# Cross-attention of a decoder layer: matmul operands padded with zeros to the full array

## Chip, cores and metric

One core of a Trainium2 chip runs the whole program. The metric is the device time in microseconds (us) of one execution; lower is better. The engines of the core run side by side and wait for each other through semaphores: TensorE (PE in the profile, its weight loads PEld), VectorE (DVE), ScalarE (ACT), GpSimd (POOL) and SyncE (SP), which issues the DMAs.

## The reference, cut to what matters

A decoder layer over 64 sequences of 128 rows and 128 features: causal self-attention, cross-attention over a context of 77 rows, and a mixture-of-experts FFN, each behind a layer norm and a residual. The change touches the cross-attention only (16 heads of 8 features):

```
Q, K, V = heads of query @ Wq.T + bq, context @ Wk.T + bk, context @ Wv.T + bv
qk      = Q @ K.T                                 # 128 x 77 per head
scores  = qk / sqrt(8)
feats   = mean(scores), mean of the row maxima, mean variance of softmax(scores)
t       = exp(clip(mlp(feats)))                   # one temperature per sequence and head
attn    = softmax(qk / (2 t))
out     = (attn @ V) @ Wo.T + bo
```

## The kernel before

The program has three stages one after the other, with a barrier between them: `self_attention`, `cross_attention` and `expert_ffn`. X, the activations of all sequences, stays on the chip. The cross stage runs a software pipeline that is unrolled: `for n in STEPS`, n from -3 to 77, the same loop on every engine, and each call in it is guarded by `real(b)`, that is 0 <= b < 64. In step n the early part works on sequence n (projections a step or two ahead), and the late part on sequence n - 11 (`LAG`), because a group of 8 sequences must pass the temperature MLP before its second softmax can start. The order on an engine is the order in which the code is written; semaphores alone tie the engines.

The parts of a step that the change touches, on TensorE:

- `scores_outer`, `scores_inner` (L1033): queries as weights, masked keys as moving data, in row groups of 32 (four heads of 8 features). They fill `SQ` with qk for the statistics.
- `subtract_max` (L1063): three more matmuls add minus the row maximum of each head onto `SQ`. Weights are `mT` (16 heads x 128 queries), the moving operand is `heads`, ones that spread each head over its 77 columns: 16 rows, and 462, 462 and 308 columns, 1232 in all.
- `by_key(b, h)` (L1074, L1078): the second softmax's scores, with keys as weights, so that the result lies key by query. Half h takes the two quads of heads 2h and 2h + 1, each in a row group of its own and in a PSUM bank of its own. First the shift, a matmul whose contraction is one row (`ones` x `shift`), then three products of 32 rows for the high and low parts of keys and queries. All have 77 columns of weights and 512 moving columns.
- `pv(b, h)` (L1092): 16 matmuls per sequence, weights `VA` (77 keys x 32 columns), moving operand the probabilities `P`, 128 columns per head.

`HK` and `LK` hold high and low parts of the keys for 16 slots, `mT` the negated maxima for 16 slots, and `P` the probabilities in four buffers. ScalarE writes `P` by `exps` (L794), `mT` by `mT_copy` (L764) and the V part of `VA` by `qkv_copy` (L760); VectorE casts `HK` (L877); GpSimd writes `LK` (L712). At the start of the stage GpSimd clears `VA` and sets its columns of ones and `ones_row`; TensorE waits for these (`const_set`, 3), computes the folded bias, which ScalarE copies, and starts the pipeline.

For comparison the self stage: its shift (L442) is a matmul over all 128 rows with a selecting matrix, its mask (L433) is a 128 x 128 matmul too, and its score products (L423) have 32 rows and 128 columns of weights. The moving operands are stored as float32 or rounded float32; a plain float32 matmul is issued as two instructions (x128 for 64 sequences), a rounded one as one.

Of the kernel before, what the change touches and what calls it, by code (L numbers as in the profile page):

```python
# [6 lines left out]
F32 = mybir.dt.float32  # L7
F32R = mybir.dt.float32r
# [8 lines left out]
TC = 77  # L17
# [506 lines left out]
def cross_attention(nc, X, ST, MEAN, RSTD, constants, loaded, dram):  # L524
# [11 lines left out]
    with ctx:  # L536
        def sb(name, shape, dt=F32):
            return ctx.enter_context(nc.sbuf_tensor("xa_" + name, shape, dt))
# [14 lines left out]
        w3r = sb("w3r", [64, 128])  # L553
        ones_row = sb("ones_row", [1, T])
        bias = sb("bias", [1, C])
        ones = sb("ones", [128, TC], F32R)
        heads = sb("heads", [H, H * TC], F32R)
        shift = sb("shift", [128, 2, JH, T], F32R)

        cx = sb("cx", [TC, 4, C])  # L560
# [2 lines left out]
        QK = sb("QK", [C, SLOTS, T + TC])  # L563
        HQ = sb("HQ", [C, QRING, T], F32R)
        LQ = sb("LQ", [C, QRING, T], F32R)
        HK = sb("HK", [C, SLOTS, TC], F32R)
        LK = sb("LK", [C, SLOTS, TC], F32R)
        VA = sb("VA", [TC, VRING, 2, PART])
        KMH = sb("KMH", [C, 2, JH, TC], F32R)
        KML = sb("KML", [C, 2, JH, TC], F32R)  # L570
        qsum = sb("qsum", [C, SLOTS])
        ksum = sb("ksum", [C, SLOTS])
        mT = sb("mT", [H, SLOTS, T], F32R)
        E1 = sb("E1", [128, 2, H * TC])
        E2 = sb("E2", [128, H * TC])
        ZS = sb("ZS", [128, 2, SLOTS * H])
# [14 lines left out]
        QMH = sb("QMH", [C, 2, JH, T], F32R)  # L591
        QML = sb("QML", [C, 2, JH, T], F32R)
        row = sb("row", [H, T], F32R)
        P = sb("P", [TC, 4, 2 * JH * T])
        o = sb("o", [128, 2 * T])
        rinv = sb("rinv", [128, H])
        on = sb("on", [128, C])
# [50 lines left out]
        rows_done = sem("rows_done")  # L648

        ALL_LOADED = 16 * len(CROSS_CONSTANTS)  # L650
        SETS = 3
        PREPARED = 6

        def real(b):
# [9 lines left out]
        def slot(b):  # L664
            return b % SLOTS
# [32 lines left out]

        @block.gpsimd
        def _(pool):  # L700
            nc.gpsimd.memset(VA[:], 0.0).then_inc(const_set, 1)
            pool.wait_ge(const_set, 1)
            units = VA[:, :, :, 0:32 * (H // 2)].rearrange("k s e (u x) -> k (s e) u x", x=32)
            nc.gpsimd.memset(units[:, :, :, DK:DK + 1], 1.0).then_inc(const_set, 1)
            nc.gpsimd.memset(ones_row[:], 1.0).then_inc(const_set, 1)
            pool.wait_ge(loaded, ALL_LOADED)
            by_head = headmask[:].unsqueeze(2)

            def low(b):
                pool.wait_ge(h_ready, 2 * b + 2)  # L710
                s, q = slot(b), b % QRING
                nc.gpsimd.tensor_tensor(LK[:, s], QK[:, s, T:T + TC], HK[:, s].bitcast(F32), ALU.subtract).then_inc(l_ready, 1)  # L712
                nc.gpsimd.tensor_tensor(LQ[:, q], QK[:, s, 0:T], HQ[:, q].bitcast(F32), ALU.subtract).then_inc(l_ready, 1)

            def key_masks(b):
                need(pool, sq_ps, b - 1)
                for part, (tile, keys) in enumerate(((KMH, HK), (KML, LK))):
                    if part == 1:
                        pool.wait_ge(l_ready, 2 * b + 1)
                    nc.gpsimd.tensor_tensor(tile[:, b % 2], keys[:, slot(b)].unsqueeze(1).to_broadcast([C, JH, TC]),  # L720
                                            by_head.to_broadcast([C, JH, TC]), ALU.mult).then_inc(km_ready, 1)

            def query_masks(b):
                need(pool, sk_ps, 2 * b - 2)
                for tile, queries, ready in ((QMH, QBH, qbh_ready), (QML, QBL, qbl_ready)):
                    pool.wait_ge(ready, b + 1)
                    nc.gpsimd.tensor_tensor(tile[:, b % 2], queries[:, b % 2].unsqueeze(1).to_broadcast([C, JH, T]),  # L727
                                            by_head.to_broadcast([C, JH, T]), ALU.mult).then_inc(qm_ready, 1)

            for n in STEPS:  # L730
                late = mlp_round(n) is not None
                if mlp_round(n - 1) is not None and real(n + 1):
                    low(n + 1)
                    key_masks(n + 1)
                if real(n - LAG + 1):
                    query_masks(n - LAG + 1)
                if real(n + 2) and not late:
                    low(n + 2)
                    key_masks(n + 2)

        @block.scalar
        def _(act):
# [5 lines left out]
            def qkv_copy(b):  # L748
                s = slot(b)
                act.wait_ge(qkv_ps, b + 1)  # L750
                need(act, qbl_ready, b - SLOTS + 1)
                need(act, group_ready, 2 * (b // GROUP) - 2)
                nc.scalar.activation(QK[:, s, 0:T], M[:, 0:T], ACT.Identity, bias=bq[:],
                                     accum_out=qsum[:, s:s + 1]).then_inc(q_sb, 1)
                nc.scalar.activation(QK[:, s, T:T + TC], M[:, T:T + TC], ACT.Identity, bias=bk[:],
                                     accum_out=ksum[:, s:s + 1]).then_inc(k_sb, 1)
                need(act, pv_ps, 2 * (b - VRING) + 2)
                v = M[0:TC, T + TC:2 * T + TC].rearrange("k (u e d) -> k e u d", e=2, d=DK)
                units = VA[:, b % VRING, :, 0:32 * (H // 2)].rearrange("k e (u x) -> k e u x", x=32)
                nc.scalar.copy(units[:, :, :, 0:DK], v).then_inc(v_sb, 1)  # L760

            def mT_copy(b):
                act.wait_ge(mT_ps, b + 1)
                nc.scalar.activation(mT[:, slot(b)], O[0:H, 2 * T:3 * T], ACT.Copy, scale=-1.0).then_inc(mT_sb, 1)  # L764

            def exp_e(b):

# [13 lines left out]
            def scaled(b):  # L781
                s = slot(b)
                act.wait_ge(cf_ready, 2 * (b // GROUP) + 2)
                need(act, qm_ready, 2 * b - 2)
                need(act, qbl_ready, b - 1)
                nc.scalar.activation(QBH[:, b % 2], QK[:, s, 0:T], ACT.Copy, scale=cfc[:, s:s + 1]).then_inc(qbh_ready, 1)  # L786
                if b > 0:
                    act.wait_ge(m_row[(b - 1) % 2], 64 * ((b - 1) // 2 + 1))
                nc.scalar.activation(row[:], mT[:, s].bitcast(F32), ACT.Copy, scale=cfh[:, s:s + 1]).then_inc(row_sb, 1)

            def exps(b, h):
                act.wait_ge(sk_ps, 2 * b + h + 1)
                need(act, pv_ps, 2 * b + h - 3)
                nc.scalar.activation(P[:, (2 * b + h) % 4, :], SK[0:TC, :], ACT.Exp).then_inc(p_ready, 1)  # L794

            def o_copy(b):
                act.wait_ge(pv_ps, 2 * b + 2)
# [16 lines left out]
            def inverse_t(r):  # L814
# [2 lines left out]
                nc.scalar.activation(CF[:], lt[:], ACT.Exp, scale=-1.0).then_inc(mlp_act, 1)  # L817

            act.wait_ge(loaded, ALL_LOADED)
            nc.scalar.activation(ones[:], ident[:, 0:TC], ACT.Copy, bias=1.0, scale=0.0).then_inc(act_set, 1)  # L820
            nc.scalar.copy(heads[:].rearrange("h (g k) -> h g k", k=TC),
                           ident[0:H, 0:H].unsqueeze(2).to_broadcast([H, H, TC])).then_inc(act_set, 1)
            act.wait_ge(bias_ps, 1)
            nc.scalar.copy(bias[:], R[0:1, 0:C]).then_inc(prepared, 1)

# [33 lines left out]
        @block.vector  # L859
        def _(dve):  # L860
            dve.wait_ge(loaded, ALL_LOADED)
            for f, scale in enumerate((1.0 / (T * TC * R8), 1.0 / (T * R8), 1.0 / T)):
                nc.vector.tensor_scalar(w1s[:, f, :], w1b[:, f, :], scale, None, ALU.mult).then_inc(prepared, 1)
            nc.vector.memset(w2p[:, 64:128], 0.0).then_inc(prepared, 1)
# [8 lines left out]
            def cast(b):  # L873
                dve.wait_ge(q_sb, b + 1)
                dve.wait_ge(k_sb, b + 1)
                need(dve, sk_ps, 2 * (b - SLOTS) + 2)
                nc.vector.tensor_copy(HK[:, slot(b)], QK[:, slot(b), T:T + TC]).then_inc(h_ready, 1)  # L877
                need(dve, sq_ps, b - QRING + 1)
                nc.vector.tensor_copy(HQ[:, b % QRING], QK[:, slot(b), 0:T]).then_inc(h_ready, 1)  # L879

# [120 lines left out]
        def _(pe):  # L1001
            mm, tr = nc.tensor.matmul, nc.tensor.transpose

            def bank(pair, a):
                return pair[:, a * JH * T:(a + 1) * JH * T]
# [61 lines left out]
            def by_key(b, h):  # L1067
                need(pe, p_ready, 2 * b + h)
                if h == 0:
                    pe.wait_ge(qm_ready, 2 * b + 2)  # L1070
                    pe.wait_ge(m_row[b % 2], 64 * (b // 2 + 1))
                quads = [(a, slice(32 * (2 * h + a), 32 * (2 * h + a) + 32), 32 * (2 * h + a)) for a in range(2)]
                for a, _, r in quads:
                    mm(bank(SK, a)[0:TC], ones[r:r + 1], shift[r:r + 1, b % 2].rearrange("c j t -> c (j t)"),  # L1074
                       start=True, stop=False)
                for part, (keys, queries) in enumerate(((HK, QMH), (HK, QML), (LK, QMH))):
                    for a, rows, _ in quads:
                        last = mm(bank(SK, a)[0:TC], keys[rows, slot(b)],  # L1078
                                  queries[rows, b % 2].rearrange("c j t -> c (j t)"), start=False, stop=(part == 2))
                last.then_inc(sk_ps, 1)  # L1080

# [739 lines left out]
```

## Time and profile before

| | |
|---|---|
| median of 3 runs | 2084.21 us (2082.62 to 2085.64) |
| the profiled execution's own time | 2087.13 us |
| its span, first to last instruction | 2085.3 us |
| TensorE busy | 1907.7 us, 91% of the span |
| VectorE, ScalarE, GpSimd busy | 1287.3, 943.2, 672.6 us |
| mean granted TensorE clock | 0.765 of full speed |
| stages by their first and last matmuls | self to 551 us, cross 563 to 1418 us, FFN from 1428 us |

How to read it: a share of busy time says that an engine has an instruction in flight, not how fast it goes. The granted clock is the share of 2.4 GHz that TensorE was given; in this trace it is only ever 1.0 or 0.5, and decimals are means over a stretch. A mean duration holds the latency of an instruction and not only the time by which it delays the next, so the distance between starts is the better measure of throughput. A shape such as 32*77 32x512 stands for 32 active rows and 77 active columns of the array, and 512 moving columns of 32 rows.

### The profile page before, as it was taken

Reading aid. Unit: us, or ns where it says so; the run is one execution under the profiler, and the core shown is the slowest. Engines: PE = TensorE matmul, PEld = TensorE weight load, DVE = VectorE, ACT = ScalarE, POOL = GpSimd, SP = SyncE. Lnnn points to the kernel's source line nnn. Section 1 sums busy time; section 2 is a strip of 40 time slices with the busy share of each in tenths; the row PEclk is TensorE's granted clock in tenths of the full one; section 3 lists DMA queues with packets and bytes.
Section 4 is the critical chain, followed back from the end, with each engine's and each line's share of the span. In section 5 each row is a group of like instructions: output and inputs, shape, how many; then the busy total and the mean of one; then the engine's idle time right before and its main releaser. Section 6 shows DMA issues by size and latency. Waiting matters only on the chain. (4 is left out here: it accounts for less than half of the span.)

```text
span 2085.3 us, 42401 instructions
## 1 busy us (share of the span) xinstructions
PE 1907.7 (91%) x14484; PEld 1419.8 (68%) x14484; DVE 1287.3 (62%) x2961; ACT 943.2 (45%) x2047; POOL 672.6 (32%) x746
## 2 busy tenths in 40 slices
PE   1999999999678999999999999995898988989888
PEld 0555555555355766676666766544898988989888
DVE  4666666666456555555555555315777777777775
ACT  1455545555345555555655565433333333333332
POOL 1344333444223333333332333221233232332322
PEclk9999999999755555555555555556999999999998
DMA  5000000000000000000000000000000000000000
GB/s 143 2 2 1 1 1 1 1 1 1 6 6 4 6 5 5 5 5 6 5 5 5 6 5 2 2 2 1 6 8 5 8 7 5 8 5 8 8 5 11
DMA packets 26229, 16.50 MB, mean 8 GB/s; under 512 B 6098, under 2 KB 23444, under 8 KB 26132
## 3 DMA queue, kind: packets, MB, share of 16 engines
q1 hardware_dynamic: 26132, 15.23, 2.7%
q8 instruction: 58, 0.95, 0.2%
q14 instruction: 39, 0.32, 0.1%
HBM read 9.97 MB, written 4.19 MB: 7 GB/s over the span
## 5 line engine op out<-in xcount | busy, mean ns | idle before, releaser
L794 ACT ACTIVATE xa_P<-xa_SK 77x1024 f32<-77x1024 f32 x128 | 130.6, 1020 | 161.0 <-PE xa_SK L1078 161.0
L280 ACT ACTIVATE sa_P<-sa_SK 128x1024 f32<-128x1024 f32 x128 | 131.2, 1025 | 149.8 <-PE sa_SK L423 149.8
L1397 ACT ACTIVATE ff_SG<-bank 128x512 f32<-128x512 f32 x128 | 76.7, 599 | 266.7 <-PE bank L1614 266.7
L353 DVE TENSOR_REDUCE sa_mx<-sa_SQ 128x8 f32<-128x1024 f32 x128 | 156.5, 1223 | 10.2 <-PE sa_SQ L423 8.7
L246 POOL TENSOR_TENSOR sa_KM<-sa_HQK,sc_headmask 128x512 fp32r<-128x512 f32 x64 | 66.6, 1041 | 297.1 <-ACT sa_HQK L275 297.1
L1519 DVE TENSOR_TENSOR ff_GU<-ff_SG,bank 128x512 f32<-128x512 f32 x128 | 87.3, 682 | 111.3 <-ACT ff_SG L1397 111.3
L1679 PE MATMUL bank<-fh_r,ff_GH 128*128 128x256 f32 x512 | 154.9, 303 | 0.0
L1612 PE MATMUL bank<-ff_ZH,fh_b 128*128 128x256 f32 x512 | 154.0, 301 | 0.0
L1614 PE MATMUL bank<-ff_ZH,fl_b 128*128 128x256 f32 x512 | 152.9, 299 | 0.0
L1613 PE MATMUL bank<-ff_ZL,fh_b 128*128 128x256 f32 x512 | 152.2, 297 | 0.0
L1680 PE MATMUL bank<-fl_r,ff_GH 128*128 128x256 f32 x512 | 152.1, 297 | 0.0
L1681 PE MATMUL bank<-fh_r,ff_GL 128*128 128x256 f32 x512 | 151.9, 297 | 0.0
L727 POOL TENSOR_TENSOR xa_QMH<-xa_QBH,xc_headmask 128x512 fp32r<-128x512 f32 x64 | 72.2, 1128 | 237.0 <-ACT xa_QBH L786 237.0
L1348 POOL TENSOR_TENSOR ff_zz<-ff_zt 128x256 f32<-128x256 f32 x32 | 23.2, 726 | 382.4 <-DVE ff_zt L1535 382.4
L886 DVE TENSOR_REDUCE xa_FEAT<-xa_SQ 128x12 f32<-128x924 f32 x64 | 71.7, 1121 | 118.6 <-PE xa_SQ L1033 118.6
L1092 PE MATMUL xa_O<-xa_P,xa_VA 77*32 77x128 f32 x2048 | 138.3, 421 | 0.0
L1525 DVE TENSOR_TENSOR ff_GL<-ff_GU,ff_GH 128x512 fp32r<-128x512 f32 x128 | 130.8, 1022 | 0.0
L712 POOL TENSOR_TENSOR xa_LK<-xa_QK,xa_HK 128x77 fp32r<-128x77 f32 x64 | 22.5, 352 | 330.0 <-DVE xa_HQ L879 330.0
L893 DVE TENSOR_REDUCE xa_ZS<-xa_E 128x16 f32<-128x1232 f32 x64 | 91.8, 1434 | 59.7 <-ACT xa_E L773 59.0
L1033 PE MATMUL xa_SQ<-xa_KMH,xa_HQ 32*128 32x308 f32 (+1 forms) x320 | 105.9, 528 | 13.6 <-ACT xa_E L773 13.6
L1356 POOL TENSOR_TENSOR ff_ZH<-ff_AH,ff_M 128x512 fp32r<-128x512 f32 x64 | 83.0, 1296 | 98.0 <-ACT ff_M L1387 98.0
L1679 PEld LDWEIGHTS bank<-fh_r,ff_GH 128*128 128x128 f32 x512 | 107.9, 211 | 0.0
(248 smaller groups left out, 5970.5 us busy)
## 6 DMA issues: line engine op xcount, KB each, us to landing
xa_shift<-xa_row SPq DMA_DIRECT2D x256, 2.0 KB
out<-X SPq DMA_DIRECT2D x64, 64.0 KB, 1.5
xa_cx<-ctx SPq DMA_DIRECT2D x64, 38.5 KB
sa_shift<-sa_mT SPq DMA_DIRECT2D x64, 8.0 KB, 1.8
fr_b<-L_ffn_B SPq DMA_DIRECT2D x2, 256.0 KB, 4.0
fr_r<-down_a SPq DMA_DIRECT2D x1, 512.0 KB, 4.9
fr_w<-L_ffn_w_gate SPq DMA_DIRECT2D x1, 256.0 KB, 3.5
fr_w<-L_ffn_w_up SPq DMA_DIRECT2D x1, 256.0 KB, 3.7
```

Source lines behind the costliest of these rows:

```text
L280: nc.scalar.activation(P[:, 2 * (k % 2) + h, :], SK[:], ACT.Exp).then_inc(p_ready, 1)
L353: nc.vector.tensor_reduce(mx[:, p, 2 * JH * h:2 * JH * h + 2 * JH], SQ[:].rearrange("q (j k) -> q j k", k=T), AX.X, ALU.max).then_inc(max_ ...
L794: nc.scalar.activation(P[:, (2 * b + h) % 4, :], SK[0:TC, :], ACT.Exp).then_inc(p_ready, 1)
L1033: return mm(SQ[:, at:at + n * TC], queries[rows, b % QRING], keys[rows, b % 2, j:j + n].rearrange("c j k -> c (j k)"), start=start, stop=stop,
L1092: last = mm(O[32 * t:32 * t + 32, h * T:h * T + T], VA[:, b % VRING].rearrange("k e x -> k (e x)")[:, 256 * e + 32 * u:256 * e + 32 * u + 32],
L1525: nc.vector.tensor_tensor(GG[1][:, k % 4, :], GU[:, k % 2, :], GG[0][:, k % 4, :].bitcast(F32), ALU.subtract).then_inc(gl_done, 1)
L1612: mm(out, w[0], x[0], start=start, stop=False, **kw)
L1613: mm(out, w[0], x[1], start=False, stop=False, **kw)
L1614: return mm(out, w[1], x[0], start=False, stop=stop, **kw)
L1679: mm(out, h, RD[0][:, f, :], start=(s == 0 and f == 0), stop=False, skip_group_check=True)
L1680: mm(out, h, RD[1][:, f, :], start=False, stop=False, skip_group_check=True)
L1681: last = mm(out, l, RD[0][:, f, :], start=False, stop=(s == 1 and f == 3), skip_group_check=True)
```

## The change

`HK`, `LK`, `ones` get 128 columns per slot instead of 77; `mT`, `heads`, `VA` and `P` get 128 rows instead of 16 or 77. The added parts are zeros, written once at the stage's start by GpSimd; writers go on writing only the real part. The matmuls of `by_key`, `subtract_max` and `pv` use the padded operands. The shift's contraction stays one row per quad. `const_set` now counts 7, and ScalarE and VectorE wait for it too. Lines that carry only `-` and `+` follow; headings of functions are left out.

```diff
-        ones = sb("ones", [128, TC], F32R)
-        heads = sb("heads", [H, H * TC], F32R)
+        ones = sb("ones", [128, T], F32R)
+        heads = sb("heads", [128, H * TC], F32R)
...
-        HK = sb("HK", [C, SLOTS, TC], F32R)
-        LK = sb("LK", [C, SLOTS, TC], F32R)
-        VA = sb("VA", [TC, VRING, 2, PART])
+        HK = sb("HK", [C, SLOTS, T], F32R)
+        LK = sb("LK", [C, SLOTS, T], F32R)
+        VA = sb("VA", [128, VRING, 2, PART])
-        mT = sb("mT", [H, SLOTS, T], F32R)
+        mT = sb("mT", [128, SLOTS, T], F32R)
...
-        P = sb("P", [TC, 4, 2 * JH * T])
+        P = sb("P", [128, 4, 2 * JH * T])
...
-        SETS = 3
+        SETS = 7
...
+            nc.gpsimd.memset(ones_row[:], 1.0).then_inc(const_set, 1)
+            nc.gpsimd.memset(HK[:].bitcast(F32), 0.0).then_inc(const_set, 1)
+            nc.gpsimd.memset(LK[:].bitcast(F32), 0.0).then_inc(const_set, 1)
+            nc.gpsimd.memset(mT[:].bitcast(F32), 0.0).then_inc(const_set, 1)
-            pool.wait_ge(const_set, 1)
-            units = VA[:, :, :, 0:32 * (H // 2)].rearrange("k s e (u x) -> k (s e) u x", x=32)
+            pool.wait_ge(const_set, 5)
+            units = VA[0:TC, :, :, 0:32 * (H // 2)].rearrange("k s e (u x) -> k (s e) u x", x=32)
-            nc.gpsimd.memset(ones_row[:], 1.0).then_inc(const_set, 1)
+            nc.gpsimd.memset(P[:], 0.0).then_inc(const_set, 1)
-                nc.gpsimd.tensor_tensor(LK[:, s], QK[:, s, T:T + TC], HK[:, s].bitcast(F32), ALU.subtract).then_inc(l_ready, 1)
+                nc.gpsimd.tensor_tensor(LK[:, s, 0:TC], QK[:, s, T:T + TC], HK[:, s, 0:TC].bitcast(F32),
+                                        ALU.subtract).then_inc(l_ready, 1)
...
-                    nc.gpsimd.tensor_tensor(tile[:, b % 2], keys[:, slot(b)].unsqueeze(1).to_broadcast([C, JH, TC]),
+                    nc.gpsimd.tensor_tensor(tile[:, b % 2], keys[:, slot(b), 0:TC].unsqueeze(1).to_broadcast([C, JH, TC]),
...
-                units = VA[:, b % VRING, :, 0:32 * (H // 2)].rearrange("k e (u x) -> k e u x", x=32)
+                units = VA[0:TC, b % VRING, :, 0:32 * (H // 2)].rearrange("k e (u x) -> k e u x", x=32)
-                nc.scalar.activation(mT[:, slot(b)], O[0:H, 2 * T:3 * T], ACT.Copy, scale=-1.0).then_inc(mT_sb, 1)
+                nc.scalar.activation(mT[0:H, slot(b)], O[0:H, 2 * T:3 * T], ACT.Copy, scale=-1.0).then_inc(mT_sb, 1)
...
-                nc.scalar.activation(row[:], mT[:, s].bitcast(F32), ACT.Copy, scale=cfh[:, s:s + 1]).then_inc(row_sb, 1)
+                nc.scalar.activation(row[:], mT[0:H, s].bitcast(F32), ACT.Copy, scale=cfh[:, s:s + 1]).then_inc(row_sb, 1)
-                nc.scalar.activation(P[:, (2 * b + h) % 4, :], SK[0:TC, :], ACT.Exp).then_inc(p_ready, 1)
+                nc.scalar.activation(P[0:TC, (2 * b + h) % 4, :], SK[0:TC, :], ACT.Exp).then_inc(p_ready, 1)
...
-            nc.scalar.activation(ones[:], ident[:, 0:TC], ACT.Copy, bias=1.0, scale=0.0).then_inc(act_set, 1)
+            nc.scalar.activation(ones[:], ident[:], ACT.Copy, bias=1.0, scale=0.0).then_inc(act_set, 1)
-                           ident[0:H, 0:H].unsqueeze(2).to_broadcast([H, H, TC])).then_inc(act_set, 1)
+                           ident[:, 0:H].unsqueeze(2).to_broadcast([128, H, TC])).then_inc(act_set, 1)
+            act.wait_ge(const_set, SETS)
...
+            dve.wait_ge(const_set, SETS)
...
-                nc.vector.tensor_copy(HK[:, slot(b)], QK[:, slot(b), T:T + TC]).then_inc(h_ready, 1)
+                nc.vector.tensor_copy(HK[:, slot(b), 0:TC], QK[:, slot(b), T:T + TC]).then_inc(h_ready, 1)
...
-                    mm(bank(SK, a)[0:TC], ones[r:r + 1], shift[r:r + 1, b % 2].rearrange("c j t -> c (j t)"),
+                    mm(bank(SK, a), ones[r:r + 1], shift[r:r + 1, b % 2].rearrange("c j t -> c (j t)"),
-                        last = mm(bank(SK, a)[0:TC], keys[rows, slot(b)],
+                        last = mm(bank(SK, a), keys[rows, slot(b)],
```

No instruction changes its place in the pipeline. On GpSimd, at the start of the cross stage, there stood before (after the branch of the stage's barrier; `xa_` marks the cross stage's tiles):

```order
L701 MEMSET xa_VA 77x7950
L704 MEMSET xa_VA 77x30x8 [waits xa_const_set]
L705 MEMSET xa_ones_row 1x128
L712 TENSOR_TENSOR xa_LK<-xa_QK,xa_HK 128x77 [waits xa_h_ready,xc_loaded]
L713 TENSOR_TENSOR xa_LQ<-xa_QK,xa_HQ 128x128
```

And now:

```order
L701 MEMSET xa_ones_row 1x128
L702 MEMSET xa_HK 128x2048
L703 MEMSET xa_LK 128x2048
L704 MEMSET xa_mT 128x2048
L705 MEMSET xa_VA 128x7950
L708 MEMSET xa_VA 77x30x8 [waits xa_const_set]
L709 MEMSET xa_P 128x4096
L716 TENSOR_TENSOR xa_LK<-xa_QK,xa_HK 128x77 [waits xa_h_ready,xc_loaded]
L718 TENSOR_TENSOR xa_LQ<-xa_QK,xa_HQ 128x128
```

Four memsets are added in front of the first real work of GpSimd, and `ones_row` went to the front.

On TensorE, in a step of the cross stage, from the transpose of the maxima to the first `pv` half, before (the shape is that of the output):

```order
L1058 MATMUL xa_O<-xc_ident,xa_FEAT 16x128 [waits xa_o_sb,xa_max_ready]
L1074 MATMUL xa_SK<-xa_shift,xa_ones 77x512 [waits xa_p_ready]
L1074 MATMUL xa_SK<-xa_shift,xa_ones 77x512
L1078 MATMUL xa_SK<-xa_QMH,xa_HK 77x512 x2
L1078 MATMUL xa_SK<-xa_QML,xa_HK 77x512 x2
L1078 MATMUL xa_SK<-xa_QMH,xa_LK 77x512 x2
L1063 MATMUL xa_SQ<-xa_heads,xa_mT 128x462 [waits xa_mT_sb]
L1063 MATMUL xa_SQ<-xa_heads,xa_mT 128x462
L1063 MATMUL xa_SQ<-xa_heads,xa_mT 128x308
L1107 MATMUL xa_R<-xc_ident,xa_on 128x128 [waits xa_o_norm]
```

And now:

```order
L1065 MATMUL xa_O<-xc_ident,xa_FEAT 16x128 [waits xa_o_sb,xa_max_ready]
L1081 MATMUL xa_SK<-xa_shift,xa_ones 128x512 [waits xa_p_ready]
L1081 MATMUL xa_SK<-xa_shift,xa_ones 128x512
L1085 MATMUL xa_SK<-xa_QMH,xa_HK 128x512 x2
L1085 MATMUL xa_SK<-xa_QML,xa_HK 128x512 x2
L1085 MATMUL xa_SK<-xa_QMH,xa_LK 128x512 x2
L1070 MATMUL xa_SQ<-xa_heads,xa_mT 128x462 [waits xa_mT_sb]
L1070 MATMUL xa_SQ<-xa_heads,xa_mT 128x462
L1070 MATMUL xa_SQ<-xa_heads,xa_mT 128x308
L1114 MATMUL xa_R<-xc_ident,xa_on 128x128 [waits xa_o_norm]
```

The order and the waits are the same; the outputs of `by_key` have 128 rows instead of 77, and the rows of the contraction, which this listing does not show, go from 16 to 128 in `subtract_max`.

## Rows read from the trace of the kernel before

**Rows 1.** the profile's page: busy tenths of TensorE and its granted clock, 40 slices
```profile
PE   1999999999678999999999999995898988989888
...
PEclk9999999999755555555555555556999999999998
```

**Rows 2.** windows: stretches inside self-attention, cross-attention, FFN, and one cross step
```profile
core 0: us, PE busy (x) PEld busy (x) DVE busy (x) ACT busy (x) POOL busy (x), PEclk, DMA share, GB/s
120.00:540.00 420.00, 418.87 (x3922) 247.70 (x3921) 284.17 (x650) 212.66 (x437) 164.05 (x162) 1.00 0.01 1
700.00:1300.00 600.00, 596.23 (x4066) 412.54 (x4062) 324.51 (x656) 347.52 (x807) 203.82 (x290) 0.50 0.02 5
1500.00:2060.00 560.00, 509.01 (x4017) 501.80 (x4016) 427.19 (x1061) 189.66 (x390) 174.20 (x140) 0.93 0.02 7
904.34:916.15 11.81, 11.81 (x84) 8.25 (x82) 6.26 (x13) 6.71 (x17) 4.22 (x6) 0.50 0.01 4
```

**Rows 3.** windows: the start of the FFN stage, before and after the clock rises
```profile
1428.40:1445.40 17.00, 9.66 (x41) 8.28 (x42) 7.13 (x25) 5.50 (x9) 5.13 (x4) 0.50 0.00 0
1445.50:1489.70 44.20, 39.14 (x332) 38.51 (x331) 35.52 (x92) 16.56 (x34) 13.19 (x10) 1.00 0.02 4
```

**Rows 4.** timeline, TensorE, self-attention's start: start us, duration us, engine, line, operation
```profile
64.59 1.42 PE L442 MATMUL sa_SK<-sa_shift,sa_pick_row 128*128 128x512 f32 x2
...
66.49 0.39 PE L423 MATMUL sa_SK<-sa_QML,sa_HQK 32*128 32x512 f32 x2
```

**Rows 5.** groups by line and shape: count | busy us, mean ns of one
```profile
L1092 PE MATMUL xa_O<-xa_P,xa_VA 77*32 77x128 f32 x2048 | 138.3, 421 | 0.0
...
L473 PE MATMUL sa_O<-sa_P,sa_VA 128*32 128x128 f32 x2048 | 82.5, 279 | 0.0
...
L1078 PE MATMUL xa_SK<-xa_QML,xa_HK 32*77 32x512 f32 x256 | 80.7, 624 | 0.0
...
L423 PE MATMUL sa_SK<-sa_QML,sa_HQK 32*128 32x512 f32 x256 | 50.4, 390 | 0.0
```

**Rows 6.** timeline, TensorE, one cross step: `by_key` half 1 with `subtract_max`
```profile
915.73 0.71 PE L1074 MATMUL xa_SK<-xa_shift,xa_ones 1*77 1x512 f32 x2
916.15 0.75 PE L1063 MATMUL xa_SQ<-xa_heads,xa_mT 16*128 16x462 f32 x1
916.24 0.63 PE L1078 MATMUL xa_SK<-xa_QMH,xa_HK 32*77 32x512 f32 x2
916.66 0.63 PE L1078 MATMUL xa_SK<-xa_QML,xa_HK 32*77 32x512 f32 x2
916.71 0.58 PE L1063 MATMUL xa_SQ<-xa_heads,xa_mT 16*128 16x462 f32 x1
917.09 0.62 PE L1078 MATMUL xa_SK<-xa_QMH,xa_LK 32*77 32x512 f32 x1
917.09 0.46 PE L1063 MATMUL xa_SQ<-xa_heads,xa_mT 16*128 16x308 f32 x1
...
917.65 0.48 PE L1107 MATMUL xa_R<-xc_ident,xa_on 128*128 128x128 f32 x1
```

**Rows 7.** weight loads by line and shape, as in rows 5
```profile
L1033 PEld LDWEIGHTS xa_SQ<-xa_KMH,xa_LQ 32*128 32x128 f32 x320 | 71.4, 328 | 0.0
...
L1078 PEld LDWEIGHTS xa_SK<-xa_QMH,xa_HK 32*77 32x77 f32 x256 | 32.2, 247 | 0.0
```

**Rows 8.** timeline, weight loads: what `by_key` half 0 waits for
```profile
907.25 0.20 PEld L1074 LDWEIGHTS xa_SK<-xa_shift,xa_ones 1*77 1x77 f32 x2 [0.38 <-ACT xa_P L794]
```

**Rows 9.** timeline, all engines, start of the cross stage
```profile
555.44 6.72 POOL L701 MEMSET xa_VA<- 77x7950 f32 x1 [28.50 <-POOLq L71]
...
562.59 0.25 POOL L705 MEMSET xa_ones_row<- 1x128 f32 x1
...
564.02 0.26 ACT L824 COPY xa_bias<-xa_R 1x128 f32<-1x128 f32 x1 [7.19 <-PE xa_R L1134]
...
564.33 0.47 PE L1014 MATMUL xa_M<-xc_ident,xa_xn 128*128 128x128 f32 x1 [0.35 <-ACT xa_bias L824]
```

## Prediction

> **What bounds the kernel now.** I read the page's slices first, then windows inside each stage, then the groups by shape, and last the timeline of one cross step. The slices [rows 1] show TensorE at nine tenths or more in most of the program, and its granted clock at nine tenths in the self and FFN stages but at five in the cross stage. The windows make this exact [rows 2]: in 120 to 540 us, inside self-attention, TensorE is busy 418.87 of 420 us at a clock of 1.00; in 700 to 1300 us, inside cross-attention, it is busy 596.23 of 600 us at 0.50. So TensorE bounds both, and in the cross stage at the lower of its two levels, 1.2 GHz. There the other engines have room: in one step of 11.81 us (904.34 to 916.15, from one first `subtract_max` matmul to the next) ScalarE is busy 6.71 us, VectorE 6.26 and GpSimd 4.22 [rows 2].
>
> What differs between the two stages is not how busy TensorE is but the shapes [rows 4 to 6]. The self stage has 128*128 matmuls of 512 columns among its 32*128 products. In the cross stage the long matmuls have 1*77, 32*77 and 16*128 active rows and columns, and `pv` has 77*32. The clock has risen twice in this trace. It rose at 66.4 us, behind two 128*128 matmuls of 512 columns and others of full shape [rows 4], and at 1445.4 us, behind an unbroken run of 128*128 matmuls [rows 3]. The change makes cross shapes larger, so it may raise the clock, and that question decides the sign.
>
> **Part 1: `subtract_max` from 16 rows to 128.** Before, it costs nothing. In [rows 6] `by_key` half 1 starts at 915.73 and its four pairs follow each other by 0.42 to 0.43 us, the time of 512 columns at 1.2 GHz. The three `subtract_max` matmuls start at 916.15, 916.71 and 917.09, in the middle of that, and the next matmul over the whole array, L1107, starts at 917.65, right behind the last `by_key` pair. `by_key` half 1 uses row groups 2 and 3, `subtract_max` row group 0 alone. With 128 rows it needs all four row groups, and can no longer run beside `by_key`. Its 1232 columns at the cadence seen (0.425 us for 512) are 1.02 us, now on the path of the engine that bounds. Part of it comes back: the `by_key` half behind it waits 0.38 us for ScalarE's exponentials [rows 8], which get more time now. Below is 1.02 - 0.38 = 0.64 us; above are the three full durations, 0.75 + 0.58 + 0.46 = 1.79 us [rows 6], if nothing overlaps. I take 0.95 us, near the cadence, since only a part of the 0.38 us delays a matmul (the weight load waits, while `pv` in front of it still drains). The overlap exists where a step has both parts, n = 11 to 63, so 53 times: 50 us, between 34 and 95.
>
> [...]
>
> **Part 2: keys and `ones` from 77 to 128 columns.** The moving columns stay 512, so the matmuls take no longer. The weight load does: a 32*77 load has a mean of 247 ns, a 32*128 load 328 ns [rows 7]. The loads run ahead under a cadence of 0.43 us, so only the first of each half, behind matmuls of another shape, can show. The means overlap in pairs, so one load of the pair grows by half of 81 ns: 0.04 us x 128 halves (64 sequences, two each) = 5 us. It is 0 if hidden, and 10 us if the whole 81 ns shows.
>
> **Part 3: `pv` from 77 to 128 rows.** The same 128 moving columns and 32 weight columns. At the lower clock the mean is 421 ns for 77 rows, and 279 ns for 128 rows in the self stage at the upper [rows 5]; 128 x 2 columns fall from 213 to 107 ns between the levels, which accounts for most of the difference and leaves none for the rows. I count 0, with no end above or below that I can find. `P` is still written on 77 rows by ScalarE.
>
> **Part 4: the start of the stage.** GpSimd clears 7950 columns of `VA` in 6.72 us [rows 9], 0.845 ns each. Added are three times 2048 columns and 4096 for `P`, 10,240 in all: 8.7 us. It ends the chain: TensorE's first matmul and, new, VectorE's preparations wait for it. Before, VectorE's preparations ran beside the memset, and TensorE's first transpose started at 564.33, 1.49 us behind the end of `ones_row` (562.84), over ScalarE's copy of the bias [rows 9]. Now VectorE's six small operations and a layer norm come behind the memset too, in about the same time; I add 0.3 us. So +9 us. Nothing covers it, since the pipeline is empty there. If `VA` takes longer by its rows (128 for 77), 4.5 us come on top: 14 us. The low end is 8.7.
>
> **Sum at the lower clock.** 50 + 5 + 9 = 64 us on the profiled execution's 2087.1: 2151. That execution is 2.9 us above the median of the runs, so 2148 as a median. With all ends together it is +43 to +119, or 2127 to 2203; the case's own range is 2127 to 2175, since the upper ends need matmuls that don't pipeline, against what every pair in [rows 6] does.
>
> **Rival 1: the clock rises, and the kernel gets faster.** Price: for like shapes, the mean at 2.4 against 1.2 GHz is 390 against 624 ns for the 512-column products, and 279 against 421 for `pv` [rows 5], or 0.63 and 0.66. Take 0.65. A step of 11.81 + 0.95 + 0.08 = 12.84 us would take 8.3 us, still above ScalarE's 6.71. The stage, 563 to 1418 us, 855 us before and 919 with my sum, takes 919/(1 + 0.54 x) if the clock is up for a share x of its time. It breaks even at x = 0.14. At a third it is 779 us, and the program takes 2008 us; at all of it 597 us and 1826 us. For it: of a step's work, the 1232 columns of `subtract_max` become full shape, and right before them stand products of 32*128 and behind them a full transpose and 16 `pv` matmuls of 128 rows, much like the stretch behind which the self stage's clock rose [rows 4]. Against it: the self stage has four 128*128 matmuls of 512 columns for the shift and four for the mask in each sequence, and the cross stage gets only 1232 columns of full shape in a step that is longer besides. The shift, 2048 columns a sequence, stays one row. And because `subtract_max` stops running beside `by_key`, the denser shapes are spread over more time, rather than packed. Zeros may not count as work either: then the change doesn't do what padding can do, which ends at my number.
>
> The Trainium skill (TensorE: Matmul & The Clock Gate, Part 1) says that the clock gate opens according to how busy the array has been of late, and closes after idle time. The trace does not bear that out if busy means an instruction in flight: 99% busy is held at 0.50 for the whole cross stage. By this rule read so, padding would change nothing of the clock, and the sum stays.
>
> **Rival 2: `subtract_max` stays hidden.** If the array lets it run ahead somewhere else, or the waits around it take all of it, the loads and the start are left: +14 us, 2098. Against it: at 99% busy there is no gap of 1 us in a step.
>
> **Rival 3: more is late than the matmuls.** `subtract_max` releases ScalarE's `exp_e`, which releases the next `scores_outer`; if that becomes the chain, a step loses up to 1.79 us and the kernel ends near 2190. Against it: `pv` and `by_key` half 0 stand between them on TensorE, and are as late.
>
> **How the numbers follow.** The clock stays low and `subtract_max` shows: 0.64, 2148 us. Rival 1: 0.24, 2008 us at a third of the stage, with wide room on both sides. Rivals 2 and 3: 0.06 each. What can be told from no change here is 0.2%, about 4 us. Slower by more: 0.64 + 0.06 + 0.06 = 0.76. Faster: rival 1 less the small part in which x is near 0.14: 0.22. Within: 0.02. The range reaches from 2030, which leaves out a bit over half of rival 1, to 2185.
>
> **What would show each step.** Clock: the granted clock in the slices of the cross stage, 0.5 or above. Part 1: the `subtract_max` matmuls start behind the last `by_key` pair instead of among them, and a step is 12.8 us. Part 2: `by_key`'s loads near 328 ns, its cadence still 0.43 us. Part 3: `pv` at 421 ns. Part 4: GpSimd's memsets end near 572 us and the first transpose starts near 573. A granted clock of 1.0 for over a seventh of the stage makes the prediction wrong, whatever the other steps do.

## The result and the profile after

The changed kernel takes 2153.57 us (median of 4 runs, 2144.31 to 2164.55) against 2083.41 us (4 runs, 2081.74 to 2085.64) beside it: ratio 1.0338, 95% interval 1.0285 to 1.0392, 70 us slower. The forecast was 2148, range 2030 to 2185. The profiled execution is the slowest of the four, 2164.55 us, 77.4 us above the one of before.

The page of the changed kernel, TensorE's busy time and its granted clock in 40 slices:

```profile
PE 1971.4 (91%) x14422; PEld 1475.5 (68%) x14484; DVE 1280.3 (59%) x2961; ACT 949.9 (44%) x2047; POOL 681.0 (31%) x750
...
PEclk9999999999555555555555555555899999999998
```

The cross stage stands at five tenths as before [rows 1]. The windows (columns as in [rows 2]) give the same inside the stage, 0.50 at 99% busy, and show the one place where the clock did rise:

```profile
core 0: us, PE busy (x) PEld busy (x) DVE busy (x) ACT busy (x) POOL busy (x), PEclk, DMA share, GB/s
...
700.00:1300.00 600.00, 596.98 (x3701) 416.78 (x3697) 294.50 (x596) 321.74 (x735) 185.50 (x265) 0.50 0.02 5
...
989.90:993.10 3.20, 2.36 (x23) 1.95 (x21) 3.07 (x6) 1.72 (x3) 3.20 (x5) 1.00 0.04 12
```

From 989.8 to 993.2 us the clock was up, the one time in the cross stage, and fell again. The four runs differ by 20 us, those of before by 4, and their mean clocks differ too: 0.757 in the slowest (2164.55), 0.769 in the fastest (2144.31), 0.763 in the two between. So stretches at the upper clock come or stay away from run to run. By the ratio of durations of 0.65 in the prediction, 20 us less takes about 37 us more at the upper clock, which is an estimate. That this makes up the whole scatter is likely, but only one execution has a trace.

One step on TensorE, against [rows 6] (start us, duration us, engine, line, operation; x3 are three matmuls in one row):

```profile
912.14 0.79 PE L1081 MATMUL xa_SK<-xa_shift,xa_ones 1*128 1x512 f32 x2
912.73 0.62 PE L1085 MATMUL xa_SK<-xa_QMH,xa_HK 32*128 32x512 f32 x2
913.16 0.62 PE L1085 MATMUL xa_SK<-xa_QML,xa_HK 32*128 32x512 f32 x2
913.59 0.62 PE L1085 MATMUL xa_SK<-xa_QMH,xa_LK 32*128 32x512 f32 x2
914.14 1.40 PE L1070 MATMUL xa_SQ<-xa_heads,xa_mT 128*128 128x462 f32 x3
915.34 0.41 PE L1114 MATMUL xa_R<-xc_ident,xa_on 128*128 128x128 f32 x1
915.68 1.08 PE L1099 MATMUL xa_O<-xa_P,xa_VA 128*32 128x128 f32 x16
916.69 0.79 PE L1081 MATMUL xa_SK<-xa_shift,xa_ones 1*128 1x512 f32 x2
```

`subtract_max` no longer starts among the `by_key` pairs but behind the last one, at 914.14, and the full transpose (L1114) follows 1.20 us later. Behind it, `pv` comes 0.34 us after the transpose instead of 0.41 (917.65 to 918.06 before), and from `pv` to `by_key` half 0 it is 1.01 us, as before (906.24 to 907.25). `by_key` half 1 takes 2.00 us to the next matmul instead of 1.92. A step went from 11.81 to 13.1 us.

Weight loads and `pv` by shape, against [rows 7] and [rows 5]:

```profile
L1085 PEld LDWEIGHTS xa_SK<-xa_QMH,xa_HK 32*128 32x128 f32 x256 | 42.7, 331 | 0.0
...
L1081 PEld LDWEIGHTS xa_SK<-xa_shift,xa_ones 1*128 1x128 f32 x256 | 36.5, 282 | 49.0 <-issue 45.2 <-ACT xa_P L799 3.8
```

```profile
L1099 PE MATMUL xa_O<-xa_P,xa_VA 128*32 128x128 f32 x2048 | 138.3, 421 | 0.0
```

The loads of 128 columns have the 330 ns forecast. `pv` has the same 421 ns with 128 rows as with 77.

The start of the stage, against [rows 9]:

```profile
556.23 0.19 POOL L701 MEMSET xa_ones_row<- 1x128 f32 x1 [28.05 <-POOLq L71]
...
556.37 1.79 POOL L702 MEMSET xa_HK<- 128x2048 f32 x1
...
561.61 6.71 POOL L705 MEMSET xa_VA<- 128x7950 f32 x1
...
568.75 3.57 POOL L709 MEMSET xa_P<- 128x4096 f32 x1
...
572.83 0.40 DVE L870 TENSOR_SCALAR xa_w1s<-xc_w1b 128x64 f32<-128x64 f32 x3 [17.07 <-POOL xa_P L709]
...
573.56 0.26 ACT L830 COPY xa_bias<-xa_R 1x128 f32<-1x128 f32 x1 [15.90 <-PE xa_R L1141]
...
573.87 0.47 PE L1021 MATMUL xa_M<-xc_ident,xa_xn 128*128 128x128 f32 x1 [0.41 <-ACT xa_bias L830]
```

The memsets run from 556.23 to 572.32, and TensorE's first transpose starts at 573.87, 9.5 us later than before, of which 0.8 us lie ahead of the stage. The whole account of the profiled execution: 0.8 ahead of the cross stage, 8.7 at its start, 69.8 within it (matmuls from 562.9 to 1417.7 us before, 854.8 us; from 572.4 to 1496.9 now, 924.6), and 1.7 us less in the FFN stage and the end, 77 in all.

### The profile page after: what moved, and what is told of

It is laid out like the page before. It is cut to its first block and busy times, and to the rows that moved or that the text cites. A ratio compares the mean times of both kernels' runs of the same rounds, so it can differ in the third digit from the quotient of the medians.

```text
span 2162.8 us, 42345 instructions
## 1 busy us (share of the span) xinstructions
PE 1971.4 (91%) x14422; PEld 1475.5 (68%) x14484; DVE 1280.3 (59%) x2961; ACT 949.9 (44%) x2047; POOL 681.0 (31%) x750
## 5 line engine op out<-in xcount | busy, mean ns | idle before, releaser
L1099 PE MATMUL xa_O<-xa_P,xa_VA 128*32 128x128 f32 x2048 | 138.3, 421 | 0.0
L1099 PEld LDWEIGHTS xa_O<-xa_P,xa_VA 128*32 128x32 f32 x2048 | 76.4, 159 | 48.9 <-issue 26.7
```

Of the source, the lines that this page charges most:

```text
L1099: last = mm(O[32 * t:32 * t + 32, h * T:h * T + T], VA[:, b % VRING].rearrange("k e x -> k (e x)")[:, 256 * e + 32 * u:256 * e + 32 * u + 32],
```

## The experiments

Each is told against runs of the kernel before on the same chip. "Clock" is the granted clock in 700 to 1200 us of the one profiled execution, inside the cross stage. Over the whole stage it is lower where it rises at all, since it stays down at both ends: 0.76 for e4, 0.73 for e5, 0.61 for e6, 0.70 for e9, 0.86 for e8, 0.87 for e11 and 0.81 for e12.

| kernel | median us (runs from to) | ratio, 95% interval | clock |
|---|---|---|---|
| changed kernel | 2153.57 (2144.31 to 2164.55) | 1.0338 (1.0285 to 1.0392) | 0.50 |
| e1_heads128 | 2145.66 (2141.96 to 2150.13) | 1.0291 (1.0268 to 1.0314) | 0.50 |
| e2_heads64 | 2155.79 (2154.51 to 2156.28) | 1.0344 (1.0327 to 1.0361) | 0.50 |
| e7_heads32 | 2084.20 (2080.93 to 2090.07) | 1.0008 (0.9995 to 1.0021) | 0.50 |
| e3_keys_pv | 2099.74 (2096.14 to 2102.35) | 1.0074 (1.0056 to 1.0093) | 0.51 |
| e4_all_shift128 | 2013.75 (1992.92 to 2015.66) | 0.9628 (0.9575 to 0.9681) | 0.89 |
| e5_nohead_shift128 | 2014.21 (2003.11 to 2030.26) | 0.9698 (0.9650 to 0.9745) | 0.84 |
| e6_all_shift32 | 2064.46 (2051.12 to 2072.91) | 0.9897 (0.9844 to 0.9950) | 0.66 |
| e9_shift128_only | 2002.83 (1999.82 to 2015.17) | 0.9637 (0.9593 to 0.9681) | 0.78 |
| e10_nohead_shift32 | 2093.23 (2084.29 to 2103.25) | 1.0062 (1.0036 to 1.0087) | 0.53 |
| e8_all_bias128 | 1946.37 (1943.52 to 1947.41) | 0.9344 (0.9314 to 0.9373) | 0.92 |
| e11_rows | 1938.06 (1906.91 to 1954.34) | 0.9320 (0.9264 to 0.9377) | 0.96 |
| e12_rows_cols | 1962.48 (1951.99 to 1976.91) | 0.9434 (0.9376 to 0.9492) | 0.88 |

**What `subtract_max` costs.** The kernel before with `mT` and `heads` of 128 rows alone:

```diff
-        heads = sb("heads", [H, H * TC], F32R)
-        mT = sb("mT", [H, SLOTS, T], F32R)
+        heads = sb("heads", [128, H * TC], F32R)
+        mT = sb("mT", [128, SLOTS, T], F32R)
+            nc.gpsimd.memset(mT[:].bitcast(F32), 0.0).then_inc(const_set, 1)
```

> The kernel before, with mT and heads alone padded to 128 rows (one memset of 2048 columns more, ScalarE waits for it). Theory (row groups): subtract_max loses its overlap with by_key half 1 and costs what stands in the changed kernel's timeline, 1.20 us less 0.07 us, in 53 steps: +60 us, and +2 us at the start of the stage: ratio about 1.030. Rival (the cost is by_key's wider weights and the chain behind it): under +20 us. The granted clock of the cross stage stays at 0.50 by both.

Measured 60 us more (2145.66 against 2085.57). Its `subtract_max` starts lie 12.95 us apart, 1.14 us more than before; 53 times that is 60. The term stands by itself.

**Why: row groups or height.** The same with 64 and with 32 in place of 128:

> As the one before, but mT and heads have 64 rows, which touches row groups 0 and 1 only, while by_key half 1 uses groups 2 and 3. Theory (row groups): the overlap stays, +2 us from the memset at the start and no more: ratio 1.001. Rival (any change of the tile's height against by_key's 32 rows drains the array): nearly as slow as with 128 rows, +50 to +60 us, ratio 1.025 or more.

> The kernel before with mT and heads at 32 rows, the height of by_key's products. With 64 rows, in row groups that by_key half 1 does not use, subtract_max lost its overlap all the same. If a change of tile height is what ends the overlap, 32 rows keep it: +2 us from the memset, ratio 1.001. Rival (any padding of mT, or the new wait of ScalarE, costs the overlap): ratio 1.03 as with 64 and 128 rows.

The theory that other row groups are enough fell. With 64 rows the kernel is 70 us slower, more than with 128. TensorE in it, columns as above:

```profile
904.00 0.71 PE L1076 MATMUL xa_SK<-xa_shift,xa_ones 1*77 1x512 f32 x2
...
905.36 0.63 PE L1080 MATMUL xa_SK<-xa_QMH,xa_LK 32*77 32x512 f32 x2
905.92 1.39 PE L1065 MATMUL xa_SQ<-xa_heads,xa_mT 64*128 64x462 f32 x3
907.24 0.47 PE L1109 MATMUL xa_R<-xc_ident,xa_on 128*128 128x128 f32 x1
907.65 1.08 PE L1094 MATMUL xa_O<-xa_P,xa_VA 77*32 77x128 f32 x16
```

The three matmuls with 64 rows use row groups 0 and 1, `by_key` half 1 uses 2 and 3, and still the first starts at 905.92, behind the last pair. With 32 rows:

```profile
899.39 0.71 PE L1076 MATMUL xa_SK<-xa_shift,xa_ones 1*77 1x512 f32 x2
899.81 0.75 PE L1065 MATMUL xa_SQ<-xa_heads,xa_mT 32*128 32x462 f32 x1
...
900.75 0.62 PE L1080 MATMUL xa_SK<-xa_QMH,xa_LK 32*77 32x512 f32 x2
...
901.30 0.47 PE L1109 MATMUL xa_R<-xc_ident,xa_on 128*128 128x128 f32 x1
```

It starts at 899.81, among the pairs, and the kernel is as fast as before. So row groups that nobody else uses do not suffice here. What ran beside the 32-row products, in other row groups, had 16 rows (before) or 32, so it lay within one row group; with 64 rows it waited for the last pair. Whether two matmuls of 64 rows would run beside each other, that is, whether equal height decides or staying within one row group, no run shows. With 128 rows `subtract_max` needs the row groups of `by_key` as well, so there both reasons hold. The 64-row form pays for two changes of height: 1.32 us to the transpose and 0.41 on to `pv`, against 1.20 and 0.34 with 128 rows, where `subtract_max` and the transpose have the same height.

The Trainium skill (TensorEngine Tiling (Array Packing), Key Properties) says that changing the tiling mode drains TensorE, while a change of tile within a mode does not. The 64-row run agrees: its first `subtract_max` starts 0.56 us behind the last `by_key` pair, where the pairs follow each other by 0.43. The prediction argued by row groups alone.

**Keys and V alone.** The changed kernel with `mT` and `heads` back at 16 rows:

```diff
-        heads = sb("heads", [128, H * TC], F32R)
-        mT = sb("mT", [128, SLOTS, T], F32R)
+        heads = sb("heads", [H, H * TC], F32R)
+        mT = sb("mT", [H, SLOTS, T], F32R)
```

> The changed kernel with mT and heads left at 16 rows: keys, ones, V and P stay padded. Theory: by_key's first loads show whole, 0.08 us in each of 128 halves = +10 us, and the start of the stage costs +7 us (four memsets of 8192 columns in all instead of 10,240): +17 us, ratio 1.008, clock 0.50 throughout the cross stage. Rival (padding raises the clock once nothing holds the matmuls apart): granted clock above 0.5 in parts of the stage and a time below before.

Measured 14 us more than before, where 17 were expected, at a clock of 0.51: in the profiled execution the clock rose twice for 3.4 us. Together with e1 this is 74 us, against 70 for the changed kernel: the parts add up.

**What is missing for the clock: the shift.** The changed kernel with the shift over 128 rows. `pick` holds a row of ones per quad in place of `ones`, and `shift` is cleared once:

```diff
-                    mm(bank(SK, a), ones[r:r + 1], shift[r:r + 1, b % 2].rearrange("c j t -> c (j t)"),
+                    mm(bank(SK, a), pick[:, r // 32], shift[:, b % 2].rearrange("c j t -> c (j t)"),
```

> The changed kernel with the shift over all 128 rows as well: weights pick one row per quad, the moving operand is the whole shift tile, cleared once. The two shift matmuls of a half no longer run side by side, at 1.2 GHz 0.43 us more per half, 0.86 us a sequence: 55 us more than the changed kernel if the clock stays at 0.50, so about 2210 us. Theory (the clock follows how much of the array the matmuls fill, zeros included): the clock is up for a good part of the cross stage and the kernel gets faster than before, 1850 to 2050 us. Rival (zeros do not count, or the shift does not matter): 2210 us, clock 0.50.

> Keys, ones, V, P and the shift (128 rows) padded, mT and heads left at 16 rows, so that subtract_max keeps its overlap with by_key half 1. Against the kernel with all of it (2014 us): 1.13 us a step at 1.2 GHz and about half of that at 2.4 GHz come back. Theory (what decides is the filled part of the array per time; subtract_max gives 1232 full columns but also takes the time of them): the clock is up for about as long, the time is 20 to 60 us below that kernel: 1950 to 1995 us. Rival (the full-shape subtract_max is what lifts the clock): the clock falls back to 0.50 in most of the stage, 2100 us or more.

> The changed kernel with the shift over the 32 rows of its quad (row group as before, rows of zeros added), so no matmul loses its overlap. It fills a quarter of the array instead of a 128th for 2048 columns a sequence. Theory (fill decides): between the changed kernel (2154 us) and the one with 128 rows (2014 us), nearer to the first, since the fill grows by a quarter of what 128 rows give: 2100 to 2150 us, with a few risen stretches. Rival (number of full-array matmuls decides): as the changed kernel, 2154 us, or 2 us more for the memset of the shift.

The window of 700 to 1200 us of these three, in that order (columns as in [rows 2]); the changed kernel has 0.50 there:

```profile
700.00:1200.00 500.00, 453.64 (x4056) 308.28 (x4056) 321.97 (x656) 343.76 (x812) 204.09 (x290) 0.89 0.02 6
```

```profile
700.00:1200.00 500.00, 450.45 (x4082) 295.71 (x4080) 325.39 (x662) 345.24 (x815) 205.88 (x294) 0.84 0.02 6
```

```profile
700.00:1200.00 500.00, 479.01 (x3609) 333.34 (x3609) 285.67 (x578) 308.91 (x717) 181.41 (x260) 0.66 0.02 5
```

With the shift of 128 rows (e4) the clock is 0.89 and the kernel is 140 us faster than the changed one, although each shift pair takes longer. In this window TensorE did 4056 matmuls, against 3070 in the changed kernel. Zeros do count: every row that was added has zeros in one operand. Nor is it only that the shift matmuls, no longer side by side, take twice the time: in e6 they still run side by side, and the clock rises. Without the padded `subtract_max` (e5) the time is the same, 2014 us, not the 20 to 60 us less that I expected: the clock fell to 0.84 and what was saved in overlap went back. With the shift of 32 rows, which keeps the overlap of the two shift matmuls (e6), the time is 2064 us; I had expected 2100 to 2150. In both, what was taken out or put in moved the clock more than I had reckoned.

**The shift alone, and the shift of 32 rows without `subtract_max`.** e9 is the kernel before with `pick` (77 columns) and the cleared `shift`, nothing else; e10 is e6 with `mT` and `heads` at 16 rows.

> The kernel before with the shift alone over 128 rows; keys, V, P and mT unpadded. Theory (the filled part of the array over time decides): not enough alone, the clock stays at 0.50 in the cross stage, and the lost side-by-side of the two shift matmuls costs 0.86 us in each of 64 sequences: +55 us, 2140 us. Rival (the shift's full-shape matmuls alone raise the clock, padding the rest is idle): below before, near the 2014 us of the kernel with everything padded.

> Everything padded but mT and heads, the shift over 32 rows: no matmul loses an overlap. At the lower clock it is the kernel with keys and V padded, 2100 us. With mT and heads padded as well it took 2064 us, at a cost of 60 us in lost overlap. Theory (fill over time; the padded subtract_max is the densest piece): without it the clock rises seldom, 2080 to 2102 us. Rival (subtract_max's padding is only a cost): 2064 less up to 60, about 2010 us.

```profile
700.00:1200.00 500.00, 459.75 (x3965) 291.94 (x3957) 315.69 (x640) 336.25 (x790) 200.12 (x287) 0.78 0.02 6
```

My theory failed on e9 and the rival holds: the shift of 128 rows alone gives 2003 us, as fast as with all the rest padded (2014). The clock is 0.78 against 0.89, but `subtract_max` keeps its overlap, loads stay short, and the start has one memset of 1024 columns more and no others. The same row of its timeline, the first shift pair of a step, at the lower and then at the upper clock (steps of 12.88 and 8.63 us):

```profile
739.98 1.20 PE L1077 MATMUL xa_SK<-xa_shift,xa_pick 128*77 128x512 f32 x2
...
752.86 1.20 PE L1077 MATMUL xa_SK<-xa_shift,xa_pick 128*77 128x512 f32 x2
```

```profile
1034.10 0.71 PE L1077 MATMUL xa_SK<-xa_shift,xa_pick 128*77 128x512 f32 x2
...
1042.73 0.71 PE L1077 MATMUL xa_SK<-xa_shift,xa_pick 128*77 128x512 f32 x2
```

At the upper clock something else comes in. TensorE is busy 12.88 of the 12.88 us in the first step, but 7.50 of 8.63 in the second, where it waits once for VectorE and once for ScalarE:

```profile
1036.76 0.69 PE L1077 MATMUL xa_SK<-xa_shift,xa_pick 128*77 128x512 f32 x2 [0.28 <-ACT xa_P L797]
...
1042.45 0.41 PE L1105 MATMUL xa_R<-xc_ident,xa_o 128*128 128x128 f32 x2 [0.84 <-DVE X L968]
```

So once the clock is up, TensorE alone no longer sets the length of a step, and these waits are part of what is left to gain.

For e10 the theory held: 2093 us at a clock of 0.53, 10 us above before. The padded `subtract_max` costs 60 us by itself, but beside the 32-row shift it lifts the clock from 0.53 to 0.66 and gains 29.

**Toward a faster kernel.** e8 is e4 with the bias matmul of the projection (L1111, one row) over 128 rows and a shorter start:

```diff
-        ones_row = sb("ones_row", [1, T])
-        bias = sb("bias", [1, C])
+        ones_row = sb("ones_row", [128, T])
+        bias = sb("bias", [128, C])
-            nc.gpsimd.memset(HK[:].bitcast(F32), 0.0).then_inc(const_set, 1)
+            nc.gpsimd.memset(HK[:, :, TC:T].bitcast(F32), 0.0).then_inc(const_set, 1)
+            nc.scalar.activation(mT[:], zero.to_broadcast([128, SLOTS, T]), ACT.Copy, scale=0.0).then_inc(act_set, 1)
```

(`LK` likewise; `P` as `mT`.)

> Everything padded, the shift over 128 rows, and two things more: the projection's bias matmul (one row before) over 128 rows, which adds full-shape matmuls for at most 0.4 us a step, and a shorter start (GpSimd clears only the added columns of HK and LK, ScalarE clears mT and P meanwhile), about 6 us less. Theory: the clock is up for a larger part of the stage, 1960 to 1995 us against 2014. Rival (the risen share does not move, the lost overlap of the bias matmul costs): 2010 to 2025 us.

1946 us, better than expected: 67 us under e4. The first matmul of the cross stage starts 6 us earlier than in e4 (565.8 against 572.2), so the rest goes with the higher clock. The two edits were not tried one by one. e12 is e8 with `mT` and `heads` of 32 rows; e11 is e12 with keys and `pick` of 77 columns:

```diff
-        HK = sb("HK", [C, SLOTS, T], F32R)
-        LK = sb("LK", [C, SLOTS, T], F32R)
-                    mm(bank(SK, a), pick[:, r // 32], shift[:, b % 2].rearrange("c j t -> c (j t)"),
+        HK = sb("HK", [C, SLOTS, TC], F32R)
+        LK = sb("LK", [C, SLOTS, TC], F32R)
+                    mm(bank(SK, a)[0:TC], pick[:, r // 32], shift[:, b % 2].rearrange("c j t -> c (j t)"),
```

> Rows padded, columns not: shift, bias matmul and pv over 128 rows, mT and heads at 32 rows (which keeps their overlap with by_key), keys and the picking weights at 77 columns, short start. The kernel before with the shift alone over 128 rows took 2003 us with 77 columns; all padded with the bias matmul took 1946 us, and paid for subtract_max at 128 rows. Theory (rows decide, columns of 77 are as good as 128; the padded subtract_max costs more than it lifts): under 1946 us, 1915 to 1940. Rival (the padded subtract_max and the columns are what keeps the clock up): 1960 to 2000 us.

> The same with keys and picking weights of 128 columns. Theory (columns gain nothing for the clock): the wider loads cost up to 0.08 us in each of 128 halves at 1.2 GHz, less at 2.4, and the start 1.4 us: 3 to 11 us slower than with 77 columns, granted clock in the stage the same. Rival (the filled columns count as the rows do): the risen share grows and it is faster by over 10 us.

```profile
700.00:1200.00 500.00, 443.47 (x4420) 280.94 (x4419) 339.66 (x702) 367.22 (x853) 216.20 (x302) 0.96 0.02 6
```

```profile
700.00:1200.00 500.00, 455.23 (x4185) 305.10 (x4184) 332.90 (x675) 351.74 (x828) 207.78 (x296) 0.88 0.02 6
```

e11 has the best median, 1938 us, 7% under before and 10% under the changed kernel, and within what was expected. Whether it beats e8 is not shown: its runs (1906.91 to 1954.34) lie on both sides of e8's (1943.52 to 1947.41). Padded columns gained nothing: e12 is 24 us slower by its median, more than the 3 to 11 for loads and start. But the two ranges of runs touch (1954.34 and 1951.99), and so do the intervals (0.9377 and 0.9376). The clocks of 0.96 and 0.88 come from one execution each, for e11 its fastest; the mean clocks of its runs go from 0.922 (1906.91 us) to 0.890 (1954.34), those of e12 from 0.900 to 0.879. So the rival, a gain of over 10 us by columns, is not borne out; that e12 is slower beyond the loads is likely and not shown, and its cause is open. Between e12 and e8, which differ in the height of `subtract_max` alone, the padded one is 16 us faster, each of its runs below each of e12's: it costs its overlap and gives more back by the clock. A kernel with 77 columns and that `subtract_max` was not tried.

## Why the prediction was right

**The clock stays at the lower level: right**, at 0.50 in the windows, but for one stretch of 3.4 us in the profiled execution. The reason given, that the shift's 2048 columns stay one row, is what the runs confirm: with them over 128 rows the clock rises (e4, e5, e9). One reading on the way was wrong: the clock of before did not rise twice but 25 times. In the FFN stage it falls to 0.50 for 3.4 us and comes back, over and over, so its 0.93 there [rows 2] is a mean. The prediction does not rest on that count, but the picture of a clock that rises once and stays is false. The other reason was half right. I took `subtract_max` to be too little for the clock; alone it is (e1: 0.50), but e6 and e10 show that it weighs.

**Part 1, `subtract_max`: the mechanism was right, the size too small, the reason wrong.** Forecast 0.95 us a step and 50 us; the timeline gives 1.20 less 0.07, or 1.13 us and 60, and e1 alone 60. The relief that I took off did not come: `by_key` half 0 starts 1.01 us behind `pv` in both. Its weight load begins 0.38 us after the one before it ended, now as before [rows 8]; only ScalarE's exponentials are no longer what it waits for:

```profile
916.69 0.28 PEld L1081 LDWEIGHTS xa_SK<-xa_shift,xa_ones 1*128 1x128 f32 x2 [0.38 <-issue]
```

That wait had been in the shadow of `pv`. Besides, the 1232 columns take 1.20 us to the transpose and not the 1.02 of their cadence; why is open. As for the reason, row groups of their own would not have saved the overlap: 64 rows lose it too (e2), 32 keep it (e7).

**Part 2, the loads: 10 us for 5.** `by_key` takes 0.08 us more in each half (2.00 for 1.92), the whole 81 ns of the pair, the upper end that I named.

**Part 3, `pv`: right**, 421 ns in both.

**Part 4, the start: right**, 8.7 us for 9. GpSimd's rate held for 128 partitions (7950 columns in 6.71 us), so the added time was that of the columns.

The sum was 64 us on the profiled execution; these terms, 60 + 10 + 9, make 79, the other stages give 0.9 back and the risen stretch perhaps 2, and 77.4 were measured. So the medians, 2148 forecast and 2153.57 measured, lie closer than the terms do, and part of that is luck: both parts that missed were too small by 15 us together, and the median is 11 us below the profiled execution, at a higher mean clock (0.763 against 0.757). The 2175 that the prediction gives as the upper end of the case is worked out nowhere; with the columns at their cadence (53 x 1.02 = 54) and the other two terms at their high ends (10 and 14) it would be 2162. Rival 1's price was near: it took 0.65 of the time for a step at the upper clock, and the two steps of e9 give 8.63/12.88 = 0.67, with the waits for VectorE and ScalarE in it, which the price left out. Rival 2 (hidden anyway) and rival 3 (more is late than the matmuls) did not come.

## What to carry to other kernels

When TensorE is busy all the time and yet at 1.2 GHz, look for its long matmuls with few rows, and try full height there first, with zeros: here one such matmul, the shift, was worth 80 us, and every padding that left it at one row was a loss or gained nothing. Before padding a small matmul, look in the timeline whether it runs beside another: here those of up to 32 rows did so in different row groups, and those of 64 and 128 rows waited. And measure a padding together with the others: what costs 60 us at the lower clock gained 29 us beside the 32-row shift, and neither gained nor lost beside the one of 128 rows (e4, e5).

## What was not expected of the hardware

- Matmuls of 64 rows in row groups 0 and 1 do not run beside matmuls of 32 rows in groups 2 and 3: 70 us over the 53 steps and the start, against 1 us with 32 rows.
- VectorE's three small operations at the start of the stage (L863) took 6.80 us beside GpSimd's memset, and 0.40 us behind it (L870 above). In e1 two small copies of VectorE took 6.72 and 6.74 us beside the same memset. So VectorE was held up by it; in the kernel before nothing waited for these operations.
- Where the clock rises only now and then, a kernel's time can scatter: 20 us over four runs for the changed kernel and 47 us for e11, against 5 us for the kernel before in the same set of runs as e11. The mean granted clock goes the same way, from 0.922 in e11's fastest run to 0.890 in its slowest. It need not be so: e8's four runs lie within 4 us.
